# Transposing raw x with centred projection weights in a one-core attention block

## The reference, cut to what matters

```python
xh  = (x - mean(x)) / sqrt(var(x) + 1e-5)          # layernorm of each row
qkv = (xh @ w_qkv).reshape(rows, 16, 24); q, k, v = split(qkv, 3)
w   = relu(q @ k.T / sqrt(8)); attn = w / (sum(w) + 1e-6)
y   = xh + (attn @ v) @ w_out + b_out
x1  = x + layernorm(y) * gamma + beta
z   = layernorm(x1)
out = x1 + sqrt((z @ cos(theta + theta_noise))**2 + (z @ sin(phi + phi_noise))**2)
```

## Time and profile before

| | us |
|---|---|
| median of 3 runs | 428.6 (428.54 to 428.6) |
| the profiled execution, its own time | 428.66 |
| its span, first to last instruction | 426.8 |
| PE busy | 415.0 |
| DVE busy | 332.9 |
| ACT busy | 339.1 |
| POOL busy | 45.9 |

### The profile page before, as it was taken

The page is one execution under the profiler, slowest core; times in us unless marked ns, Lnnn a source line. Parts: engine busy times, 40 slices in busy tenths (PEclk is TensorE's granted clock), DMA queues, the critical chain, the costliest instruction groups (busy, mean ns, idle before and its releaser), DMA issues.

```text
span 426.8 us, 9025 instructions
## 1 busy us (share of the span) xinstructions
PE 415.0 (97%) x3294; PEld 122.9 (29%) x3294; DVE 332.9 (78%) x659; ACT 339.1 (79%) x595; POOL 45.9 (11%) x57
## 2 busy tenths in 40 slices
PE   7899999999999999999999999999999999999985
PEld 6333222222222322222222322222222322222244
DVE  6775778777688898777778898777778898777857
ACT  2767878788788888888888888888888888888843
POOL 4794000000000000000101000000100000000201
PEclk9999999999999999999999999999999999999999
DMA  5117841001012100101011100101012000000200
GB/s 166 25 51 148 162 111 51 2 8 43 2 51 56 26 26 13 39 2 51 26 53 54 26 27 16 35 2 51 26 51 55 2 27 2 25 2 29 66 0 26
DMA packets 11134, 17.42 MB, mean 41 GB/s; under 512 B 3092, under 2 KB 4756, under 8 KB 10708
## 3 DMA queue, kind: packets, MB, share of 16 engines
q1 hardware_dynamic: 10948, 16.70, 14.6%
q10 hardware_dynamic: 144, 0.13, 0.2%
HBM read 3.86 MB, written 5.10 MB: 21 GB/s over the span
## 4 chain that ended last, share of the span: by engine, by line
PE 93%; DVE 3%; ACT 2%; DMA 1%; POOL 0%; issue 0%; DVEq 0%
PE pv L996 59%; PE sc L961 27%; PE pv L1051 1%; PE pv L893 1%; PE pv L902 1%; PE pv L914 1%; DMA x_sb<-x_dram 1%; PE pv L1022 1%; ACT w_buf L536 0%; PE pv L1003 0%; DVE stats L640 0%; ACT w_buf L533 0%; DVE x L782 0%; PE sc L1051 0%; PE sc L1003 0%
## 5 line engine op out<-in xcount | busy, mean ns | idle before, releaser
L996 PE MATMUL pv<-w_buf,v_sb 128*32 128x512 f32 x2048 | 272.4, 604 | 0.0
L686 DVE TENSOR_SCALAR w_buf<-sc 128x512 f32<-128x512 f32 x256 | 176.9, 691 | 73.8 <-PE sc L961 64.9
L533 ACT ACTIVATE w_buf<-sc 128x512 f32<-128x512 f32 x256 | 153.1, 598 | 67.0 <-PE sc L961 66.5
L536 ACT ACTIVATE w_buf<-sc 128x512 f32<-128x512 f32 (+1 forms) x256 | 183.7, 718 | 0.0
L961 PE MATMUL sc<-q_rep,k_rep 32*128 32x512 f32 x1024 | 134.0, 494 | 2.3 <-ACT w_buf L533 0.9
L690 DVE TENSOR_SCALAR w_buf<-sc 128x512 f32<-128x512 f32 x182 | 123.8, 680 | 1.3 <-PE sc L961 1.3
L961 PEld LDWEIGHTS sc<-q_rep,k_rep 32*128 32x128 f32 x1024 | 52.4, 181 | 216.6 <-ACT w_buf L533 175.9
L996 PEld LDWEIGHTS pv<-w_buf,v_sb 128*32 128x32 f32 x2048 | 40.4, 108 | 66.5 <-ACT w_buf L536 34.1
L451 POOL TENSOR_TENSOR oT<-o_raw,o_scale 128x512 f32<-128x512 f32 (+1 forms) x4 | 5.1, 1282 | 164.6 <-DMA o_scale<-inverse_dram 100.7
L467 POOL TENSOR_TENSOR mag<-sq 128x256 f32<-128x256 f32 x6 | 4.4, 730 | 77.5 <-ACT sq L571 77.5
L457 POOL TENSOR_TENSOR x<-x,mv 128x512 f32<-128x512 f32 (+1 forms) x5 | 4.4, 885 | 71.2 <-DVE x L782 71.2
(11 more groups left out here) (104 smaller groups left out, 136.1 us busy)
## 6 DMA issues: line engine op xcount, KB each, us to landing
pv_dram<-pv_sb SPq DMA_DIRECT2D x15, 256.0 KB, 2.0
q_rep<-q_hi SPq DMA_DIRECT2D x30, 64.0 KB, 2.1
q_rep<-q_lo SPq DMA_DIRECT2D x30, 64.0 KB, 2.1
k_rep<-k_hi SPq DMA_DIRECT2D x6, 256.0 KB, 4.1
k_rep<-k_lo SPq DMA_DIRECT2D x6, 256.0 KB, 5.3
x_sb<-x_dram SPq DMA_DIRECT2D x3, 256.0 KB, 3.9
o_raw<-pv_dram SPq DMA_DIRECT2D x3, 256.0 KB
o_scale<-inverse_dram SPq DMA_DIRECT2D x3, 256.0 KB
```

The lines of the kernel that those rows point to most:

```text
L533: nc.scalar.activation(w_buf[:, s % W_STEPS, 0, :], early[:, 0, :], ACT.Relu).then_inc(relu[0], 1)
L536: nc.scalar.activation(w_buf[:, s % W_STEPS, 2:2 + n, :], late[:, 0:n, :], ACT.Relu).then_inc(relu[0], 1)
L686: nc.vector.tensor_scalar(w_buf[:, s % W_STEPS, 1, :], early[:, 1, :], 0.0, None, ALU.max).then_inc(relu[1], 2 if both else 1)
L996: last = nc.tensor.matmul(bank[32 * i:32 * i + 32, :], v_sb[:, k, HPG * g + i, :], w_buf[:, s % W_STEPS, i, :], start=(k == 0), stop=(k == ...
```

## The change

- PE transposes the raw x (x_sb) as soon as it has landed, and no longer the normalised xn. The mean is taken out by the weights: a new matrix `centring` = ident - averager is multiplied into w_qkv on PE (128x384 into sc[2]), and DVE copies the result to w_rep and w3 (`take_weights`), which POOL did before.
- q and k so stay unscaled. V rows are multiplied by 1/(var + eps) in `take_v` (four ACT instructions with a scale), and the column of ones becomes 1/sqrt(var + eps), an ACT square root broadcast to 16 heads. The guard on the sum is multiplied by the deviation of the query row: POOL makes eps_std, PE transposes it (16 rows) in ffn_means, DVE copies it, SP stores it to DRAM and loads it spread out (five DMAs in pass 0 ahead of the group-3 queries).
- `statistics` is split: `variance` runs apart; chunk 2 and 3 statistics and variances move into the hooks of pass 0. The roots move to ACT hooks (0,12) and (0,13).
- POOL: the three pads of V after rep_ready; then after the last root eps_std, normalise_x of all four chunks, memset of o_sb, L433, L438, L441, in this order.
- Warm-up 8 instead of 12, on `averager`, which DVE now writes first; step 4 instead of step 1 is in FIRST_BOTH_LATE.

```diff
-WARM_UP = 12
+WARM_UP = 8
-FIRST_BOTH_LATE = ((1, 11, 13, 15), ...
+FIRST_BOTH_LATE = ((4, 11, 13, 15), ...
@@ SP, pass 0
+                        if c == 0 and g == G - 1:
+                            sp.wait_ge(eps_T_ready, 1)
+                            sp.dma_start(eps_dram[:, :], eps_T[:, :]).then_inc(eps_saved, 16)
+                            sp.wait_ge(eps_saved, 16)
+                            for j in range(NC):
+                                sp.dma_start(eps_spread[:, j, :], ...).then_inc(eps_loaded, 16)
@@ POOL
+                nc.gpsimd.tensor_tensor(centring[:, :], ident[:, :], averager[:, :],
+                                        ALU.subtract).then_inc(centring_ready, 1)
-                    nc.gpsimd.memset(v_sb[:, :, heads, HD:HD + 1], 1.0).then_inc(v_pad, 1)
...
-                normalise_x(1)
-                normalise_x(2)
-                pad_v(1)
-                normalise_x(3)
-                for g in range(2, G):
+                pool.wait_ge(rep_ready, 2)
+                for g in range(1, G):
                     pad_v(g)
-                nc.gpsimd.memset(averager[:, :], 1 / D).then_inc(averager_ready, 1)
+                pool.wait_ge(rstd_ready, NC)
+                nc.gpsimd.tensor_tensor(eps_std[:, :], var_eps[:, :], rstd[:, :], ALU.mult).then_inc(std_ready, 1)
+                pool.wait_ge(std_ready, 1)
+                nc.gpsimd.tensor_scalar(eps_std[:, :], eps_std[:, :], DEN_EPS, None,
+                                        ALU.mult).then_inc(eps_std_ready, 1)
+                for c in range(NC):
+                    normalise_x(c)
                 nc.gpsimd.memset(o_sb[:, :, 0:(G - 1) * HPG * HD], 0.0).then_inc(o_zero, 1)
@@ ACT take_v
-                    nc.scalar.copy(v_sb[:, chunk(c), :, 0:HD], ...).then_inc(v_ready, 1)
+                    act.wait_ge(var_ready, c + 1)
+                    nc.scalar.activation(v_sb[:, chunk(c), :, HD],
+                                         inv_var[:, chunk(c)].unsqueeze(2).to_broadcast([P, TPC, H]), ACT.Sqrt)
+                    for t in range(TPC):
+                        n = c * TPC + t
+                        last = nc.scalar.activation(v_sb[:, n, :, 0:HD], ..., ACT.Copy, scale=inv_var[:, n:n + 1])
@@ DVE
+                def take_weights():
+                    centred_w = sc[2][:, 1, 0:3 * D].rearrange("p (h c d) -> p c h d", h=H, c=3)
+                    dve.wait_ge(w_centred, 1)
+                    for n in (1, 0):
+                        nc.vector.tensor_copy(w_rep[:, n, :]..., centred_w[:, n, 0:HPG]...).then_inc(w_rep_ready, 1)
+                    nc.vector.tensor_copy(w3[:, :, :]..., centred_w).then_inc(w3_ready, 1)
                 statistics(0)
-                normalise_x(0)
+                take_weights()
                 statistics(1)
-                statistics(2)
+                variance(0)
                 low_rows_of(k_rep[:, 0, 0:CW], k_head, sc[1][:, 0, :], 1, k_head_ready)
                 low_rows_of(q_rep[:, 0, :], q_head, pv[0][:, :], 0, q_head_ready)
+                variance(1)
@@ DVE pass 0 hooks
-                run_pass(0, [((0, 0), lambda: take_k(1)), ((0, 1), lambda: statistics(3)),
+                run_pass(0, [((0, 0), lambda: take_k(1)), ((0, 1), lambda: statistics(2)),
+                             ((0, 2), lambda: variance(2)), ((0, 4), lambda: statistics(3)),
+                             ((0, 8), lambda: variance(3)),
@@ PE
-                pe.wait_ge(ident_ready, 1)
-                warm_up(WARM_UP)
-                transpose_first()
+                pe.wait_ge(averager_ready, 1)
+                warm_up(WARM_UP)
+                pe.wait_ge(ident_ready, 1)
+                transpose_first()
+                pe.wait_ge(centring_ready, 1)
+                pe.wait_ge(wqkv_loaded, 16)
+                nc.tensor.matmul(sc[2][:, 1, 0:3 * D], centring[:, :], wqkv_sb[:, :], start=True,
+                                 stop=True).then_inc(w_centred, 1)
+                transpose_x(1)
                 pe.wait_ge(xT_ready, 2)
                 project_rep(1, sc[1][:, 0, :])
                 project_rep(0, pv[0][:, :])
-                transpose_x(1)
@@ PE ffn_means
+                    pe.wait_ge(eps_std_ready, 1)
+                    nc.tensor.transpose(pv[0][0:NT, 2 * D:2 * D + P], eps_std[:, :],
+                                        ident[:, :]).then_inc(means_done, 1)
```

More of the change, by code:

```diff
@@ L138, in block_kernel @@
         rstd = sb("rstd", [P, NT])
+        var_eps = sb("var_eps", [P, NT])
+        eps_std = sb("eps_std", [P, NT])
+        centring = sb("centring", [P, P])
+        eps_T = sb("eps_T", [NT, P])
+        eps_spread = sb("eps_spread", [P, NC, H * CW // P])
+        eps_dram = nc.dram_tensor("eps_dram", [NT, P], F32).ap()
         stats_p = sb("stats_p", [P, TPC, 6])
@@ L160, in block_kernel @@
         rows_own = sem("rows_own")
-        xn_tile = sem("xn_tile")
+        w_centred = sem("w_centred")
+        centring_ready = sem("centring_ready")
+        std_ready = sem("std_ready")
+        eps_std_ready = sem("eps_std_ready")
+        eps_saved = sem("eps_saved")
+        eps_T_ready = sem("eps_T_ready")
+        eps_loaded = sem("eps_loaded")
         rep_done = sem("rep_done")
@@ L173, in block_kernel @@
         ln_own = sem("ln_own")
+        stats_own = sem("stats_own")
         var_ready = sem("var_ready")
@@ L375, in _ @@
                     for g in range(G if c < NC - 1 else G - 1):
+                        if c == 0 and g == G - 1:
[3 more added lines that the diff above has]
+                            for j in range(NC):
+                                sp.dma_start(eps_spread[:, j, :],
+                                             eps_dram[chunk(j), :].rearrange("t (u b) -> (t u) b", u=2)
+                                             .unsqueeze(0).to_broadcast([H, HD, H * CW // P])
+                                             ).then_inc(eps_loaded, 16)
                         if c < NC - 1:
@@ L393, in _ @@
                                         base=0, pattern=[[-1, P]], channel_multiplier=1).then_inc(ident_ready, 1)
+                pool.wait_ge(ident_ready, 1)
+                pool.wait_ge(averager_ready, 1)
+                nc.gpsimd.tensor_tensor(centring[:, :], ident[:, :], averager[:, :],
+                                        ALU.subtract).then_inc(centring_ready, 1)
                 def pad_v(g):
@@ L508, in take_v @@
                     act.wait_ge(v_done, c + 1)
-                    nc.scalar.copy(v_sb[:, chunk(c), :, 0:HD],
-                                   v_bank[c].rearrange("p (t h d) -> p t h d", t=TPC, h=H)).then_inc(v_ready, 1)
+                    act.wait_ge(var_ready, c + 1)
[3 more added lines that the diff above has]
+                        n = c * TPC + t
+                        last = nc.scalar.activation(v_sb[:, n, :, 0:HD],
+                                                    v_bank[c][:, t * P:(t + 1) * P].rearrange("p (h d) -> p h d", h=H),
+                                                    ACT.Copy, scale=inv_var[:, n:n + 1])
+                    last.then_inc(v_ready, 1)
                 def take_head(head, bank, n, ready):
@@ L516, in _ @@
                 act.dma_start(x_sb[:, 2:TPC, :], x_v[:, 2:TPC, :]).then_inc(x_second, 16)
-                root(0)
+                act.wait_ge(ident_ready, 1)
+                nc.scalar.activation(spare_act[:, :], ident[:, 0:1], ACT.Sqrt)
                 for half in range(2):
@@ L521, in _ @@
                     nc.scalar.copy(xT[:, cols], xT_bank[0][:, half, 0:2 * P]).then_inc(xT_ready, 1)
-                root(1)
+                take_xT(1)
                 take_head(k_head, sc[1][:, 0, :], 0, k_head_ready)
-                root(2)
                 take_head(q_head, pv[0][:, :], 1, q_head_ready)
                 take_v(0)
-                take_xT(1)
                 def relu_step(c, s):
@@ L598, in run_pass @@
                                     hook()
-                run_pass(0, [((0, 0), lambda: take_k(1)), ((0, 1), lambda: take_xT(2)), ((0, 2), lambda: root(3)),
+                run_pass(0, [((0, 0), lambda: take_k(1)), ((0, 1), lambda: take_xT(2)),
                              ((0, 2), lambda: take_v(1)), ((0, 3), lambda: take_k(2)), ((0, 4), lambda: take_xT(3)),
@@ L603, in _ @@
                              ((0, 8), lambda: take_v(2)), ((0, 10), lambda: take_v(3)),
+                             ((0, 12), lambda: root(0)), ((0, 12), lambda: root(1)),
+                             ((0, 13), lambda: root(2)), ((0, 13), lambda: root(3)),
                              ((1, 8), lambda: take_q(1)), ((2, 8), lambda: take_q(2)),
@@ L626, in _ @@
                 rows = Own(dve, rows_own)
+                nc.vector.memset(averager[:, :], 1 / D).then_inc(averager_ready, 1)
                 dve.wait_ge(ident_ready, 1)
@@ L640, in statistics, with variance @@
                         last = nc.vector.bn_stats(stats[:, t, :], x_sb[:, t, :])
-                    own(last)
```

(41 more changed lines are left out.)

14 lines of the change are left out of this document (9 added, 5 removed).

## The result

The change makes the kernel slower: 432.0 us median (430.54 to 432.09, 5 runs) against 428.6, ratio 1.0067, 95% interval 1.0051 to 1.0083. The forecast was 431.3. The runs fall into two groups, 430.54 and 430.65 at a mean granted clock of 0.997 and 0.998, and 432.0 to 432.09 at 0.990 and 0.991.

What follows compares the result with a forecast made beforehand. PE, busy 97% of the span, was taken to bound the kernel. Head -1.5, later delays +0.15, collision +3.85, eps_std transpose +0.15, tail adds +0.05 summed to +2.7 on 428.6: 431.3 us, range 428.8 to 432.4.

Steps and rivals of the forecast that it cites:

- The head: First 17.6 us, before PE's steady steps: first score 1.5 us earlier, 1.35 remaining after 0.15 for later delays.
- three pads of V ... wait for rep_ready ... : nothing: POOL's pads, 1.32 us each, end near 14.6, long before group 1, so their later start costs nothing.
- The 0.15 allowed for take_v and the roots: Extra ACT work and statistics(2), variance(2) in pass 0 take 0.15 us off the head's gain, between 0 and 0.6.
- POOL's timetable: POOL's moved residual work in pass 0 starts near 41.5 us and ends at 64.9, beside DVE's trig parts.
- The collision: Trig parts from 59.1 us: DVE instructions wait for POOL's; relu 28 starts 2.5 us later, a loss of 3.85.
- the two cases that the price was read from: Trace: L633 took 1.02 us beside POOL's memset; one L782 took 0.70 beside L457, against under 0.3 each.
- the first rival: Trig parts: only the first of a pair waits, relu 29 is 1.3 to 1.7 late; +1.8, 430.4 us; chance 0.2.
- L730 needs L729's semaphore, so POOL's last instruction gets in: End of the trig parts: L730 waits for POOL's last instruction and ends at 66.55 us, +1.3.
- the transpose of eps_std: Extra PE transpose, taken as one L882: +0.15 us.
- The third rival: Head gives nothing, as DVE's copies or a later rise of PE's clock use it up: 432.6 us; chance 0.08.
- The second rival: DVE's trig parts in pass 0 don't wait for POOL: -1.15, 427.4 us; chance 0.16.

Runs made afterwards that it cites:

- e5: Changed kernel with DVE's trig parts at steps 30 to 36 of pass 0 and POOL's V pads waiting for variance(1): 426.7 us, ratio 0.9953.
- e3: Changed kernel with POOL's three V pads waiting for var_ready 2 instead of rep_ready 2: 430.32 us, ratio 1.0036.
- e7: Changed kernel with POOL's eight adds waiting for angles_ready, trig parts left at steps 25 to 31: 427.79 us, ratio 0.9975.
- e1: Changed kernel with DVE's seven trig parts moved from steps 25 to 31 of pass 0 to steps 30 to 36: 427.48 us, ratio 0.9967.
- e2: Kernel before with one more wait: POOL starts its residual work only after the score of step 21: 431.7 us, ratio 1.0064.
- e8: Kernel before with DVE's trig parts at steps 30 to 36 of pass 0: 428.85 us, ratio 1.0001.
- e10: 6 warm-up matmuls instead of 8 in e5's kernel: 426.57 us, ratio 0.9949.
- e4: Changed kernel with 12 warm-up matmuls instead of 8: 432.5 us, ratio 1.0086.

## Why the prediction was right

**The head: right in kind, 0.2 to 0.3 too much.** The prediction had 1.5 us at the first score and 1.35 left at PE; the profile has 1.24 (12.10 to 10.86 for the first L1013) and 1.16 at the first values. Several terms were off and partly cancel. In the chain PE is 0.8 late at the end of the centring matmul (6.98 against 6.2): the warm-up ended at 4.83 instead of 4.3, and the matmul, taken as 0.9, took 1.49. DVE then needed 3.83 to the end of the low rows, 0.5 less than its terms. The matmul's two records took 0.85 each, against 0.49 in e5's profiled run, where the pair took 0.81 and the first score came at 10.06, 2.0 earlier than before. That is like the values at a granted clock of 0.50, 1.86 against 0.99; but the profile gives a granted clock of 1.00 for this stretch, in both kernels, so the lower level is inferred here from the spacing. And "three pads of V ... wait for rep_ready ... : nothing" was wrong. The sentence looked at whether the pads are done in time for group 1, and not at what DVE does beside them. L677 is of the kind that the prediction itself had found in L633, a one-input tensor_scalar from SBUF to SBUF. DVE paid 0.9 us for it, and PE 0.4: in e3, without the wait, the first value product is 1.57 earlier than before (17.61 to 16.04), and so more than the 1.35 forecast. The 0.15 allowed for take_v and the roots does not show as a loss there.

**POOL's timetable: right.** 41.5 was forecast for its start and it was 41.60; for its end 64.9, with the waits "65 or 66", and it was 65.21. Adding up one engine's own rows, instruction by instruction behind the event that now releases it, was enough.

**The collision: mechanism shown, size 1.0 to 1.1 too large.** Forecast was a loss of 3.85 there; the profiled run has 2.76 against before and 2.85 against e7. One of the two cases that the price was read from was misread: L782 alone lasts 0.34 (four in a row start 0.28 apart), not under 0.3, so its wait was 0.36. L765 waited 0.5 instead of 0.9, since DVE came 0.3 later than computed and so nearer to POOL's next boundary; L768 waited 0.3 instead of 0.65; L769 waited 1.1 for a whole POOL instruction, as forecast and against the first rival, which had it slip in behind L768. The step that failed is "L730 needs L729's semaphore, so POOL's last instruction gets in": L772 (L729) waited 1.0 for POOL's last instruction, and L773 (L730) then found POOL idle and took 0.29. One wait instead of a small one and a whole one. e1, e7 and e2 take the collision away from either side and put it into the old kernel; e8 shows that the place alone is worth nothing.

**Why the median still lies near the forecast: in part by luck.** The sum with the measured terms is -1.16 for the head, 0.12 of its gain lost again before step 25, 2.76 for the collision, 0.11 for the transpose of eps_std (L1093 in the chain, forecast 0.15), and about 0.24 spread over passes 1 to 3 that I did not follow: 2.1, the difference of the spans. That is 430.65, and 432.0 is 1.4 more. The prediction knew no such term at that place. A group of runs at a clock of 0.990 is there in the changed kernel and in e3, and e2's profiled run shows what one of e2's looks like: 433.46 where the other four took 431.59 to 431.75. The windows of e2:

```profile
62.00:63.00 1.00, 0.42 (x4) 0.21 (x2) 1.00 (x3) 0.68 (x2) 1.00 (x2) 1.00 0.45 129
63.00:64.00 1.00, 1.00 (x10) 0.16 (x8) 1.00 (x1) 0.60 (x1) 1.00 (x1) 1.00 0.62 236
64.00:65.00 1.00, 0.54 (x6) 0.21 (x3) 0.97 (x3) 0.41 (x1) 1.00 (x2) 1.00 0.00 0
65.00:66.00 1.00, 1.00 (x6) 0.49 (x10) 1.00 (x2) 0.35 (x2) 1.00 (x2) 0.50 0.00 0
...
70.00:71.00 1.00, 1.00 (x8) 0.29 (x4) 0.12 (x1) 0.00 (x0) 0.00 (x0) 0.50 0.00 0
71.00:72.00 1.00, 1.00 (x12) 0.20 (x8) 0.55 (x1) 0.65 (x2) 0.00 (x0) 0.59 0.00 0
```

PE, held up by the collision, is busy for 0.42 and 0.54 of two of the microseconds before; then its clock is at 0.50 for almost 7 us, and its chain has values of 1.86 us instead of 0.99. This costs 1.8 us after the collision is over. That the group of the changed kernel at 432 is the same is likely and not shown: its profiled run was of the other group. For it are its 0.990 and its 1.4 us, and the count: a mean clock of 0.990 or 0.991 is there in 5 of 15 runs of the changed kernel, e2 and e3, which have the collision, and in none of the 47 of e1 and e5 to e10, which do not (e4 has both waits, and 0.992 to 0.994). So the median came near the forecast because a collision sized 1.1 too large made up for a clock term that was missing.

**The third rival** put the clock only into the rise after the shorter warm-up. It does come late in some runs (L977 at 1.49 in the changed kernel, 0.81 in e5 with the same warm-up), for 0.8 us at the first score, and does not keep the head from gaining. With the 12 warm-up matmuls of before (e4) the first score is not earlier, 11.01. The second rival, no wait and 427.4, is what the kernel does once POOL is out of the way: e1 at 427.5 and e7 at 427.8.

## What to carry to other kernels

When work of an engine with time to spare is moved, lay out its new timetable and look at every instruction of the neighbour that shares its way into SBUF, not only at the moment when its results are due: here POOL work that nobody waited for cost 2.8 us and more, because DVE reads two SBUF tensors, or runs SBUF-to-SBUF scalar instructions, beside it. The bill is at most one POOL instruction for each such DVE instruction (here three of the four that ran beside POOL's adds paid 0.5 to 1.1 and one, L768, 0.3), and PE pays it as far as DVE is the one it waits for: nearly all at the trig parts, 0.4 of 0.9 at L677. Shifting either side is enough: it turned a loss of 0.67% into a gain of 0.25 to 0.33%, and with the pads shifted too into 0.47%.

## What the runs showed of the hardware

- The exclusion of DVE and POOL holds for a four-element instruction as for a large one: L677 took 1.08 us beside a memset of 128x1472 and 0.17 without it, though its input takes only every second element and POOL's instruction reads nothing. The relus and L684, with at most one SBUF input and one from PSUM, took 0.66 to 0.69 beside any of it. The Trainium skill ("SBUF — State Buffer", Who interferes with whom) draws the same line, and the runs agree. One record of before is less clear: L645, of L677's kind, took 0.19 at 10.15, while POOL's L415 is shown from 9.28 to 10.32; the ends of POOL's spans are rough.
- I had not expected PE's clock to fall in the middle of dense work. It did in e2 at 65 us for nearly 7 us, in e4 between 15 and 19, and in e1's profiled run from 14 to 18, where the values took 1.87; in the five microseconds before, PE was never idle for more than 0.6 us at a time. What sets it off is not shown: PE in the changed kernel's profiled run has a gap of 0.99 us at 65.6, and is busy for 0.53, 0.63 and 0.38 of single microseconds around it, at a granted clock of 1.00 throughout. The Trainium skill ("TensorE: Matmul & The Clock Gate", HAM oscillation — how this bites in real kernels) warns of idle gaps between bursts of matmuls; here the falls came behind short gaps, and only in some executions of the same kernel. In e2's profiled run a stall was thus followed by a slow stretch that cost 1.8 us more.
- PE's first closely spaced records come at different times in executions with the same warm-up: the same matmul took 1.49 us in the changed kernel and 0.81 in e5, where it starts at 5.48 and 5.35, and 0.88 in e1, where it starts at 4.90.
